# Graph attention layer: the pieces of a step stand in another order on TensorE, ScalarE and VectorE

## The chip, the cores and the metric

One NeuronCore of a Trainium2 chip runs the whole kernel. The metric is the device time of one execution in microseconds (us).

## The reference

Four graph layers run one after the other on 50,000 nodes of 128 features and 25,000 edges, sorted by their target. After each layer the result is added to the input and normalised. The change lies in the third layer, graph attention with four heads. For every edge, and for a self loop at every node:

```
x_l, x_r = x @ W_l + b_l, x @ W_r + b_r
m = leaky_relu(x_l[src] + x_r[tgt] + edge_weight @ W_e, 0.2)
logits = einsum('ehc,hc->eh', m, att)
ex = exp(logits - segment_max(logits, tgt)[tgt])
alpha = ex / (segment_sum(ex, tgt)[tgt] + 1e-16)
out = gelu(segment_sum(alpha * x_l[src], tgt) + bias)
h = out + x;  out = (h - mean) * rsqrt(var + eps) * ln_w + ln_b
x = layernorm(x + out)
```

## The kernel before

Each layer is a function with a program of its own for each engine; all engines meet at its end. `layer2` is the attention layer. It works on 49 tiles (`STEPS`) of 512 edges and, beside them, 49 tiles of 1024 nodes (two blocks of 512). Its loop counts steps `c` from 0 to 62 on each engine. In step `c` the engines handle edge and node tile `c` freshly gathered, node tile `g1 = c-1` and `g2 = c-2` in the later parts of the normalisation, and, 11 steps behind (`lag`), edge tiles `e0 = c-11`, `e1 = c-12`, `e2 = c-13`, whose attention weights are known by then. So there are three regimes: steps 0 to 11 without the edge tail (the ramp), steps 13 to 48 with everything, and steps 49 to 62 with the edge tail alone (the drain). Every seven tiles form a run, whose softmax is done in two steps: `s1` in steps 8, 15, 22, ..., 50 (`running_maximum`, `maximum_between_chunks`, `exponents`) and `s2` one step later (`running_sum`, `sum_between_chunks`, `weights`).

Every engine executes its program strictly in the order in which it is written, and waits on semaphores for the others. The order inside a step is written out by hand. In this document the pieces have these names; the line is that of the profile.

TensorE (PE): V, the value products of both edge ends (L1394, L1395, into psZ); A, the logits (L1405, L1406, into psA); TN, turning the node tile (L1361 from xn, into psT); EN and EE, centring of the gelu results of nodes and edges (L1366 into psP and psU); T1N and T1E, turning the normalised rows of nodes and edges (L1361 from n, into psT and psU); ZR and ZS, the products for the logits (L1444, L1446, into psZ); FN and FE, the second centring (L1366 into psP and psU); TE, turning the edge rows of the next tile (L1361 from xd_xs, into psT); Y, the node product (L1475, into psP). The run steps add small products into psA: m_rows, m_cols (s1), d_rows, d_cols (s2).

ScalarE (ACT): G and GE, gelu of nodes and edges (L1496, L1501, with a table load ahead); nodeT (L1505), values (L1509), alike (L1514), a table load back (L1516), affn and affe (L1520, L1525), sq (L1534), low (L1538), Exp (L1543, run steps), edgeT (L1486), lnv (L1549), rstd (L1553).

VectorE (DVE): N1, the scaling (L1567); W, S and AGG, weighting, adding and scanning of values (L1680, L1682, L1685); P1N and P1E, the residual additions that read EN and EE (L1694, L1699); ZW (L1711); VAR, the row sums (L1571); P2N and P2E, the additions that read FN and FE (L1728, L1746); Z, ZSL, ZL, the inputs of the logits (L1734, L1738, L1741).

The order of a step before:

```
PE   V A TN EN EE [m_rows d_rows] T1N T1E ZR ZS [m_cols d_cols] FN FE TE Y
ACT  G GE nodeT values alike table affn affe sq low [Exp] edgeT lnv rstd
DVE  N1 [max sum] W S AGG P1N P1E [between chunks] ZW VAR [exponents weights] P2N Z ZSL ZL P2E
```

The DMA queue of SyncE loads the edge weights, xn, share (each head's attention weights, spread over 32 partitions) and x2e, and stores logits, pre2 and shares. It is in order too: xn of tile c+1 waits for P2N of step c-1, share for AGG, the logits for alike. GpSimd gathers xd_xs, two tiles ahead of TE. `wait(eng, sem, n)` is a semaphore wait that is left out while n is not positive.

Of the kernel before, what the change touches and what calls it, by code (L numbers as in the profile page):

```python
# [20 lines left out]
P = 128  # L21
NODES, EDGES = 50000, 25000
TILE = 512
# [1187 lines left out]
def layer2(nc, io, h):  # L1211
# [4 lines left out]
    with ExitStack() as ctx:  # L1216
# [5 lines left out]
        lag, ring, runs = 11, 12, 7  # L1222
# [51 lines left out]
        def blocks_of(g):  # L1274
            return 0 if is_tile(g) else 2, 3 if is_tile(g - lag) else 2

        def is_group(g):
            return 0 <= g < STEPS + lag

        def run_at(c, behind):  # L1280
            s, k = divmod(c - behind, runs)
            return s if k == 0 and 0 <= s < runs else None
# [17 lines left out]
        def _(sp):  # L1300
# [15 lines left out]
            for c in range(ends):  # L1316
                if is_tile(c + 1):
                    load_weights(c + 1)
                    load_nodes(c + 1)
# [24 lines left out]
                g3, e3 = c - 3, c - 3 - lag  # L1344
# [13 lines left out]
        def _(pe):  # L1358
# [28 lines left out]
            for c in range(ends):  # L1387
                now, last = is_tile(c), is_tile(c - 1)
                g1, g2, e1, e2 = c - 1, c - 2, c - 1 - lag, c - 2 - lag
# [7 lines left out]
                if last:  # L1397
                    pe.wait_ge(zl_ready, c)
                    pe.wait_ge(zsl_ready, c)
                    wait(pe, a_kept, c - 1)  # L1400
                    done = (c - 1 - runs - 1) // runs + 1
                    wait(pe, m_cols, done)
                    done = (c - 1 - runs - 2) // runs + 1
                    wait(pe, d_cols, done)
                    nc.tensor.matmul(psA[0:36, 0, :], att_a[:, :], zl[:, :], start=True, stop=False)  # L1405
                    nc.tensor.matmul(psA[0:36, 0, :], att_s[:, :], zsl[:, :], start=False, stop=True).then_inc(a_ready, 1)  # L1406
                if now:
                    pe.wait_ge(node_landed[c % 4], 16 * (c // 4 + 1))
                    for k in range(2):
                        ins = turned_rows(psT[:, k, :], xn[:, c % 4, k, :])  # L1410
                    ins.then_inc(n_turned, 1)
# [9 lines left out]
                s = run_at(c, runs + 1)  # L1421
                if s is not None:
                    pe.wait_ge(top_done, s + 1)
                    pe.wait_ge(a_kept, min(c, STEPS))
                    rows_of(psA[:, 0, :], [m_here[:, chunk - 1:chunk]]).then_inc(m_rows, 1)
                s = run_at(c, runs + 2)
                if s is not None:
                    pe.wait_ge(sums_done, s + 1)
                    pe.wait_ge(a_kept, min(c, STEPS))
                    rows_of(psA[:, 0, :], [c_here[:, chunk - 1:chunk], d_here[:, chunk - 1:chunk]]).then_inc(d_rows, 1)  # L1430
                if is_group(g2):
                    pe.wait_ge(n1_ready, g2 + 1)
                if is_tile(g2):
                    pe.wait_ge(n_kept, min(c + 1, STEPS))
                    wait(pe, affn_ready, g2)
                    for k in range(2):
                        ins = turned_rows(psT[:, k, :], n1[:, k, :])
                    ins.then_inc(n1n_turned, 1)
                if is_tile(e2):
                    pe.wait_ge(pre1e_ready, min(e1 + 1, STEPS))  # L1440
                    turned_rows(psU[:, 0, :], n1[:, 2, :]).then_inc(n1e_turned, 1)
                if now:
# [3 lines left out]
                    nc.tensor.matmul(psZ[:, 1, :], h.w_lr[:, :], edgeT[:, c % 2, 0, :],  # L1446
                                     start=True, stop=True).then_inc(zs_ready, 1)
                s = run_at(c, runs + 1)
                if s is not None:
                    pe.wait_ge(m_lined, s + 1)  # L1450
                    nc.tensor.matmul(psA[:, 0, P:P + 1], m_line[:, :], ones[:, :], start=True, stop=True).then_inc(m_cols, 1)
                s = run_at(c, runs + 2)
                if s is not None:
                    pe.wait_ge(d_lined, s + 1)
                    nc.tensor.matmul(psA[:, 0, 2 * P:2 * P + 1], d_line[:, :], ones[:, :],
                                     start=True, stop=True).then_inc(d_cols, 1)
# [6 lines left out]
                if is_tile(e2):  # L1463
                    pe.wait_ge(affe_ready, e2 + 1)
                    centred(psU[:, 0, :], affT[:, 2, :]).then_inc(fe_ready, 1)
                if is_tile(c + 1):
                    pe.wait_ge(n_kept, c + 1)
                    wait(pe, affn_ready, g2 + 1)
                    turn_edges(c + 1)
                if now:  # L1470
                    pe.wait_ge(n_kept, c + 1)
                    wait(pe, pre1n_ready, g1 + 1)
                    wait(pe, pre2n_ready, g2 + 1)
                    for k in range(2):
                        ins = nc.tensor.matmul(psP[:, k, :], h.w["w_l"][:, :], nodeT[:, c % 2, k, :],  # L1475
                                               start=True, stop=True)
                    ins.then_inc(y_ready, 1)

        @block.scalar
        def _(act):  # L1480
# [9 lines left out]
            for c in range(ends):  # L1490
                now, last = is_tile(c), is_tile(c - 1)
                g1, g2, e1, e2 = c - 1, c - 2, c - 1 - lag, c - 2 - lag
# [9 lines left out]
                if now:  # L1502
                    act.wait_ge(n_turned, c + 1)
                    wait(act, y_ready, c - 1)
                    nc.scalar.activation(nodeT[:, c % 2, :, :], psT[:, :, :], ACT.Copy).then_inc(n_kept, 1)  # L1505
# [5 lines left out]
                if last:  # L1511
                    act.wait_ge(a_ready, c)
                    wait(act, alike_stored[(c - 1) % 2], 32 * ((c - 1) // 2))
                    nc.scalar.activation(alike[:, (c - 1) % 2, :], psA[0:36, 0, :], ACT.Copy).then_inc(a_kept, 1)  # L1514
# [7 lines left out]
                if is_tile(e2):  # L1522
                    act.wait_ge(n1e_turned, e2 + 1)
                    wait(act, ee_ready, min(e1 + 1, STEPS))
                    nc.scalar.activation(affT[:, 2, :], psU[:, 0, :], ACT.Identity, bias=h.col("ln_b"),  # L1525
                                         scale=h.col("ln_w")).then_inc(affe_ready, 1)
                if is_group(g1):
                    a, b = blocks_of(g1)
# [5 lines left out]
                    nc.scalar.activation(sq1[:, a:b, :], pre1[:, a:b, :], ACT.Square).then_inc(sq1_ready, 1)  # L1534
                if now:
# [4 lines left out]
                s = run_at(c, runs + 1)  # L1540
                if s is not None:
                    act.wait_ge(args_ready, s + 1)
                    nc.scalar.activation(expo[:, :, :], expo[:, :, :], ACT.Exp).then_inc(exps_ready, 1)  # L1543
                if is_tile(c + 1):
                    keep_edges(c + 1)
                if is_group(g1):
# [3 lines left out]
                                         scale=1.0 / P).then_inc(lnv1_ready, 1)  # L1550
                    act.wait_ge(lnv1_ready, g1 + 1)
                    wait(act, n1_ready, g1)
                    nc.scalar.activation(rstd1[:, 4 * a:4 * b], lnv1[:, 4 * a:4 * b], ACT.Exp,  # L1553
                                         scale=-0.5).then_inc(rstd1_ready, 1)

        @block.vector
        def _(dve):
# [104 lines left out]
            for c in range(ends):  # L1662
                now = is_tile(c)
                g1, g2, e0, e1, e2 = c - 1, c - 2, c - lag, c - 1 - lag, c - 2 - lag
                if is_group(g2):
                    a, b = blocks_of(g2)
# [3 lines left out]
                    scaled(n1[:, a:b, :], pre1[:, a:b, :], rstd1[:, 4 * a:4 * b], b - a, n1_ready)  # L1670
                s = run_at(c, runs + 1)
                if s is not None:
                    running_maximum(s)
                s = run_at(c, runs + 2)
                if s is not None:
                    running_sum(s)
                if is_tile(e0):
# [3 lines left out]
                    dve.wait_ge(weighed, e0 + 1)  # L1681
                    nc.vector.tensor_tensor(v[:, 0, :], v[:, 0, :], v[:, 1, :], ALU.add).then_inc(summed, 1)  # L1682
                    dve.wait_ge(summed, e0 + 1)
                    wait(dve, ge_ready, e0 - 1)
                    nc.vector.tensor_tensor_scan(agg[:, e0 % 2, :], share[:, e0 % 2, 0, :], v[:, 0, :],  # L1685
                                                 0.0 if e0 == 0 else agg[:, 1 - e0 % 2, TILE - 1:TILE],
                                                 ALU.mult, ALU.add).then_inc(agg_ready, 1)
                if is_group(g1):
                    wait(dve, n1_ready, g1)
                    wait(dve, sq1_ready, g1)  # L1690
                if is_tile(g1):
# [4 lines left out]
                if is_tile(e1):  # L1696
                    dve.wait_ge(ee_ready, e1 + 1)
                    dve.wait_ge(x2e_landed[e1 % 4], 16 * (e1 // 4 + 1))
                    nc.vector.tensor_tensor(pre1[:, 2, :], psU[:, 0, :], x2e[:, e1 % 4, :],  # L1699
                                            ALU.add).then_inc(pre1e_ready, 1)  # L1700
                s = run_at(c, runs + 1)
                if s is not None:
                    maximum_between_chunks(s)
# [381 lines left out]
```

## Time and profile before

| | |
|---|---|
| median of 3 runs | 3335.7 us (3334.68 to 3337.22) |
| the profiled execution | 3335.34 us, span 3333.5 us |
| attention layer | about 1797 to 2775 us of the span |
| mean granted TensorE clock | 0.903 |

Times in the rows are microseconds from the start of the span. A row of the timeline gives start, duration, engine, line, what is written from what, the number of instructions merged, and in brackets the idle time before it with what ended it. The duration of a group of matmuls includes the end of the last one; from the start of one group to the start of the next is what the engine needs for it. PEclk is the share of full speed (2.4 GHz) that the throttle granted.

### The profile page before, as it was taken

How to read it: one execution, taken by the hardware profiler on the slowest of the kernel's cores; microseconds unless marked ns; L12 is line 12 of the kernel's file. 1: busy time of each engine (PE TensorE's matmuls, PEld its weight loads, DVE VectorE, ACT ScalarE, POOL GpSimd, SP SyncE). 2: the span in 40 equal slices, each digit the busy share in tenths (PEclk: the TensorE clock that was granted, in tenths of full speed). 3: DMA queues.
4: the chain of work that ended last, by engine and by line, in shares of the span. 5: the costliest groups of instructions: out<-in, count | busy, mean ns of one | idle time of the engine just before them, and what ended most of it. 6: DMA issues, size and time to landing. Idle time of an engine off the chain costs nothing. (4 is left out here: it accounts for less than half of the span.)

```text
span 3333.5 us, 45939 instructions
## 1 busy us (share of the span) xinstructions
PE 2612.3 (78%) x14227; PEld 1767.1 (53%) x14227; DVE 2674.7 (80%) x3290; ACT 2007.4 (60%) x3334; POOL 1912.3 (57%) x1771
## 2 busy tenths in 40 slices
PE   7899999869999968888886989999999853435510
PEld 3466666646666646656654556666666642224300
DVE  6599999969999969999995467788778765999910
ACT  0177777646556649899895666666766653545500
POOL 4477777433333337777773555555555105777776
PEclk9999999989999989999997999999999955566855
DMA  7467667556666647777774456776776656985211
GB/s 209 111 191 221 221 220 222 190 179 199 201 197 198 198 152 230 229 235 231 230 237 122 121 147 172 191 181 178 193 183 178 161 130 194 280 275 172 84 39 40
DMA packets 495084, 611.76 MB, mean 184 GB/s; under 512 B 66866, under 2 KB 284652, under 8 KB 494717
## 3 DMA queue, kind: packets, MB, share of 16 engines
q1 hardware_dynamic: 433030, 495.63, 49.1%
q0 software_dynamic: 56480, 111.88, 12.7%
q8 instruction: 118, 1.93, 0.2%
q10 hardware_dynamic: 5334, 1.32, 0.2%
q14 instruction: 122, 0.99, 0.1%
HBM read 391.94 MB, written 220.55 MB: 184 GB/s over the span
## 5 line engine op out<-in xcount | busy, mean ns | idle before, releaser
L1294 POOL DMA_INDIRECT g_xd_xs<-table_x,dst_row x196 | 227.8, 1162 | 338.8 <-PE g_psT L1361 245.7
L1801 POOL DMA_INDIRECT f_rows<-table_x,src_row x196 | 229.2, 1169 | 231.9 <-POOLq L1216 172.5
L775 POOL DMA_INDIRECT c_xs<-table_x,src_row x196 | 185.4, 946 | 303.4 <-PE c_psT L916 250.2
L765 POOL DMA_INDIRECT c_xs<-table_h,src_row x196 | 220.5, 1125 | 120.5 <-issue 78.4
L497 POOL DMA_INDIRECT xs<-in_x,src_i x196 | 227.1, 1159 | 86.5 <-issue 55.5
L482 POOL DMA_INDIRECT xd<-in_x,dst_i x196 | 216.6, 1105 | 94.8 <-issue 47.9
L1294 POOL DMA_INDIRECT g_xd_xs<-table_x,src_row x196 | 221.0, 1128 | 59.8 <-issue 59.8
L1808 POOL DMA_INDIRECT out<-f_rows,end_i x196 | 197.4, 1007 | 62.5 <-issue 62.5
L1853 PE MATMUL f_psT<-w_ident,f_rows 128*128 128x128 f32 x196 | 48.7, 395 | 220.3 <-DVE f_rows L1946 220.3
L765 POOL DMA_INDIRECT c_xd<-table_h,dst_row x196 | 185.8, 948 | 59.8 <-issue 59.8
L1366 PEld LDWEIGHTS g_psP<-w_center,g_turns 128*128 128x128 f32 x1568 | 185.5, 192 | 26.6 <-ACT g_turns L1520 13.1
L1571 DVE TENSOR_REDUCE g_var<-g_sq 128x12 f32<-128x1536 f32 (+2 forms) x60 | 87.6, 1460 | 139.1 <-ACT g_sq L1534 136.4
L1366 PE MATMUL g_psP<-w_center,g_turns 128*128 128x128 f32 x1568 | 194.2, 277 | 5.8 <-ACT g_turns L1520 5.8
L1023 ACT ACTIVATE c_xo<-c_pre,c_rstd 128x128 f32<-128x128 f32 x588 | 181.9, 388 | 1.6
L1853 PEld LDWEIGHTS f_psT<-w_ident,f_rows 128*128 128x128 f32 x196 | 31.0, 195 | 233.1 <-DVE f_rows L1946 233.1
L1366 PE MATMUL g_psU<-w_center,g_turns 128*128 128x128 f32 x784 | 125.2, 311 | 34.7 <-ACT g_turns L1501 23.3
L1694 DVE TENSOR_TENSOR g_pre<-g_psP,g_xn 128x1024 f32<-128x1024 f32 x49 | 60.0, 1224 | 107.4 <-PE g_psP L1366 107.4
L1070 ACT ACTIVATE c_xnT<-c_psT 128x512 f32<-128x512 f32 x196 | 111.5, 599 | 40.6 <-PE c_psT L916 40.2
L1505 ACT ACTIVATE g_nodeT<-g_psT 128x1024 f32<-128x1024 f32 x49 | 50.2, 1024 | 141.6 <-PE g_psT L1361 141.6
L1366 PEld LDWEIGHTS g_psU<-w_center,g_turns 128*128 128x128 f32 x784 | 112.5, 221 | 41.9 <-ACT g_turns L1501 28.8
L946 PE MATMUL c_psV<-c_xsT,w_v 128*128 128x512 f32 x196 | 105.8, 622 | 35.6 <-DVE c_pv L1162 35.6
L1877 ACT ACTIVATE f_sqe<-f_rows 128x512 f32<-128x512 f32 x49 | 30.8, 629 | 166.9 <-DVE f_vare L1923 146.5
(333 smaller groups left out, 8643.8 us busy)
## 6 DMA issues: line engine op xcount, KB each, us to landing
g_share<-shares SPq DMA_DIRECT2D x196, 192.0 KB
xn<-in_x SPq DMA_DIRECT2D x49, 512.0 KB
table_x<-xo SPq DMA_DIRECT2D x49, 512.0 KB
table_x1b<-xb SPq DMA_DIRECT2D x49, 512.0 KB, 4.9
c_xn<-table_x SPq DMA_DIRECT2D x49, 512.0 KB
table_h<-c_xo SPq DMA_DIRECT2D x49, 512.0 KB
c_xn<-table_h SPq DMA_DIRECT2D x49, 512.0 KB
c_x1r<-table_x1b SPq DMA_DIRECT2D x49, 512.0 KB
```

Source lines behind the costliest of these rows:

```text
L482: pool.indirect_dma_start(out=quarters(h.xd0[:, s, :])[j], out_offset=None, in_=io["x0"], in_offset=edge_index(h.dst_i, n, j)).then_inc(h. ...
L497: pool.indirect_dma_start(out=quarters(h.xs0[:, s, :])[j], out_offset=None, in_=io["x0"], in_offset=edge_index(h.src_i, n, j)).then_inc(h. ...
L765: pool.indirect_dma_start(out=quarters(rows[:, s, :])[j], out_offset=None, in_=table, in_offset=edge_index(columns, now.n, j)).then_inc(la ...
L775: pool.indirect_dma_start(out=quarters(xs[:, s, :])[j], out_offset=None, in_=table, in_offset=edge_index(h.src_row, now.n, j)).then_inc(sr ...
L946: nc.tensor.matmul(psV[:, :], w_v[:, :], xsT[:, now.slot, :], start=True, stop=True).then_inc(v_ready, 1)
L1023: ins = nc.scalar.activation(quarters(xo[:, g.slot, j // 4, :])[j % 4], quarters(pre[:, g.slot, j // 4, :])[j % 4], ACT.Copy, scale=rstd[: ...
L1070: nc.scalar.activation(xnT[:, s, k, :], psT[0 if spread else k][:, :], ACT.Copy).then_inc(turned_sb, 1)
L1294: pool.indirect_dma_start(out=quarters(xd_xs[:, s, k, :])[j], out_offset=None, in_=table, in_offset=edge_index(columns, now.n, j)).then_in ...
L1366: ins = nc.tensor.matmul(o, x, h.w["center"][:, :], start=True, stop=True)
L1571: nc.vector.tensor_reduce(var, by_row(sq.rearrange("p b n -> p (b n)")), AX_X, ALU.add).then_inc(ready, 1)
L1801: pool.indirect_dma_start(out=quarters(rows[:, n, :])[j], out_offset=None, in_=table, in_offset=edge_index(h.src_row, n, j)).then_inc(src_ ...
L1808: pool.indirect_dma_start(out=io["out"], out_offset=edge_index(h.end_i, n, j), in_=quarters(rows[:, n, :])[j], in_offset=None, bounds_chec ...
```

## The change

The same instructions are issued in another order. `behind` is 0, so `d` is `c`, `lead` is `lag`, and which tile is handled in which step stays.

```
PE   V TN EN EE T1N ZR A FN T1E ZS [m_rows d_rows] TE FE [m_cols] Y [d_cols]
ACT  G GE nodeT values table affn sq alike affe low lnv edgeT rstd [Exp]
DVE  N1 W [max sum] P1N ZW P1E Z S ZL VAR P2N [between chunks] ZSL [exponents] AGG P2E [weights]
```

Waits that were implied by the old order are written out: TN waits for edgeT and affn (readers of psT), T1E for N1, TE for affn; A waits for `args_ready` and `shares_ready` (VectorE has read psA) where it waited for `m_cols` and `d_cols` (TensorE has written it); ZL waits for A of its own step. The core of the diff:

```diff
-        lag, ring, runs = 11, 12, 7
+        lag, ring, runs, behind = 11, 12, 7, 0
+        lead = lag - behind
...
@@ sync @@
                 if is_tile(c + 1):
                     load_weights(c + 1)
-                    load_nodes(c + 1)
+                if is_tile(c + 1 - behind) and c + 1 > behind:
+                    load_nodes(c + 1 - behind)
...
@@ tensor @@
-                if last:
-                    pe.wait_ge(zl_ready, c)
-                    pe.wait_ge(zsl_ready, c)
-                    wait(pe, a_kept, c - 1)
...
-                    wait(pe, m_cols, done)
...
-                    wait(pe, d_cols, done)
-                    nc.tensor.matmul(psA[0:36, 0, :], att_a[:, :], zl[:, :], start=True, stop=False)
-                    nc.tensor.matmul(psA[0:36, 0, :], att_s[:, :], zsl[:, :], start=False, stop=True).then_inc(a_ready, 1)
-                if now:
-                    pe.wait_ge(node_landed[c % 4], 16 * (c // 4 + 1))
+                if is_tile(d):
+                    pe.wait_ge(node_landed[d % 4], 16 * (d // 4 + 1))
+                    pe.wait_ge(e_kept, min(c + 1, STEPS))
+                    wait(pe, affn_ready, min(g2, STEPS))
...
-                if is_tile(e2):
-                    pe.wait_ge(pre1e_ready, min(e1 + 1, STEPS))
-                    turned_rows(psU[:, 0, :], n1[:, 2, :]).then_inc(n1e_turned, 1)
                 if now:
                     pe.wait_ge(v_kept, c + 1)
                     nc.tensor.matmul(psZ[:, 0, :], h.w["w_r"][:, :], edgeT[:, c % 2, 0, :],
                                      start=True, stop=True).then_inc(z_ready, 1)
...
+                if last:
+                    pe.wait_ge(zl_ready, c)
+                    pe.wait_ge(zsl_ready, c)
+                    wait(pe, a_kept, c - 1)
...
+                    wait(pe, args_ready, done)
...
+                    wait(pe, shares_ready, done)
+                    nc.tensor.matmul(psA[0:36, 0, :], att_a[:, :], zl[:, :], start=True, stop=False)
+                    nc.tensor.matmul(psA[0:36, 0, :], att_s[:, :], zsl[:, :], start=False, stop=True).then_inc(a_ready, 1)
...
                 if is_tile(e2):
+                    pe.wait_ge(n1_ready, g2 + 1)
+                    pe.wait_ge(pre1e_ready, min(e1 + 1, STEPS))
+                    turned_rows(psU[:, 0, :], n1[:, 2, :]).then_inc(n1e_turned, 1)
+                if now:
+                    pe.wait_ge(v_kept, c + 1)
+                    nc.tensor.matmul(psZ[:, 1, :], h.w_lr[:, :], edgeT[:, c % 2, 0, :],
+                                     start=True, stop=True).then_inc(zs_ready, 1)
...
+                if is_tile(c + 1):
+                    wait(pe, n_kept, min(d + 1, STEPS))
+                    wait(pe, affn_ready, min(g2 + 1, STEPS))
+                    turn_edges(c + 1)
+                if is_tile(e2):
                     pe.wait_ge(affe_ready, e2 + 1)
                     centred(psU[:, 0, :], affT[:, 2, :]).then_inc(fe_ready, 1)
...
@@ vector @@
+                if now:
+                    dve.wait_ge(z_added, c + 1)
+                    wait(dve, a_ready, c)
+                    nc.vector.scalar_tensor_tensor(out=zl[:, :], in0=z[:, :], scalar=0.2, in1=z[:, :],
+                                                   op0=ALU.mult, op1=ALU.max).then_inc(zl_ready, 1)
                 if is_group(g1):
...
                     sums(var1[:, 4 * a:4 * b], sq1[:, a:b, :], var1_ready)
...
+                if is_tile(e0):
+                    v = values[:, e0 % ring, :, :]
+                    dve.wait_ge(summed, e0 + 1)
+                    wait(dve, ge_ready, e0 - 1)
+                    nc.vector.tensor_tensor_scan(agg[:, e0 % 2, :], share[:, e0 % 2, 0, :], v[:, 0, :],
```

The rest of the diff moves the other pieces to the places shown in the order above, with their waits.

## Rows read from the trace of the kernel before

**Rows 1.** Windows: stretch, length, busy PE, PEld, DVE, ACT, POOL, PEclk, DMA share, GB/s.
```profile
2010.00:2620.00 610.00, 571.74 (x3236) 381.70 (x3237) 477.99 (x583) 419.55 (x492) 327.67 (x272) 1.00 0.72 182
2660.00:2772.00 112.00, 64.11 (x258) 51.96 (x258) 67.61 (x99) 55.00 (x77) 0.00 (x0) 0.53 0.43 113
```

**Rows 2.** Timeline of TensorE, two neighbouring plain steps, from T1E to T1N.
```profile
2217.21 0.66 PE L1361 MATMUL g_psU<-w_ident,g_n 128*128 128x128 f32 x4 [0.32 <-DVE g_pre L1699]
2217.70 1.02 PE L1444 MATMUL g_psZ<-g_edgeT,w_w_r 128*128 128x512 f32 x2
...
2219.42 1.95 PE L1366 MATMUL g_psP<-w_center,g_turns 128*128 128x128 f32 x16
...
2222.10 1.04 PE L1361 MATMUL g_psT<-w_ident,g_xd_xs 128*128 128x128 f32 x8
...
2223.49 1.96 PE L1475 MATMUL g_psP<-g_nodeT,w_w_l 128*128 128x512 f32 x4 [0.36 <-DVE g_pre L1728]
...
2225.36 1.10 PE L1394 MATMUL g_psZ<-g_edgeT,w_w_l 128*128 128x512 f32 x2
...
2227.25 1.05 PE L1405 MATMUL g_psA<-g_zl,g_att_a 128*36 128x512 f32 x2
...
2229.09 1.09 PE L1361 MATMUL g_psT<-w_ident,g_xn 128*128 128x128 f32 x8
...
2230.01 1.95 PE L1366 MATMUL g_psP<-w_center,g_turns 128*128 128x128 f32 x16
...
2231.80 1.06 PE L1366 MATMUL g_psU<-w_center,g_turns 128*128 128x128 f32 x8
...
2232.70 1.04 PE L1361 MATMUL g_psT<-w_ident,g_n 128*128 128x128 f32 x8
```

**Rows 3.** Timeline of ScalarE and VectorE in the same two steps.
```profile
2217.19 1.21 ACT L1520 ACTIVATE g_turns<-g_psT,cols 128x1024 f32<-128x1024 f32 x1
...
2218.95 1.48 ACT L1534 ACTIVATE g_sq<-g_pre 128x1536 f32<-128x1536 f32 x1
...
2220.46 1.75 DVE L1571 TENSOR_REDUCE g_var<-g_sq 128x12 f32<-128x1536 f32 x1 [2.65 <-ACT g_sq L1534]
...
2224.58 0.68 DVE L1741 SCALAR_TENSOR_TENSOR g_zl<-g_z 128x512 f32<-128x512 f32 x1
```

**Rows 4.** Waits from 2005 to 2625 us: total, times, longest.
```profile
DVE g_var L1571 <- ACT g_sq L1534: 86.4, 36, 2.7
...
PE g_psP L1475 <- DVE g_pre L1728: 31.4, 35, 2.6
```

**Rows 5.** Timeline: V of steps 2, 8, 22 and 24.
```profile
1838.51 1.10 PE L1394 MATMUL g_psZ<-g_edgeT,w_w_l 128*128 128x512 f32 x2 [1.49 <-DVE g_zl L1741]
...
1930.29 1.10 PE L1394 MATMUL g_psZ<-g_edgeT,w_w_l 128*128 128x512 f32 x2
...
2170.06 1.10 PE L1394 MATMUL g_psZ<-g_edgeT,w_w_l 128*128 128x512 f32 x2
...
2208.52 1.10 PE L1394 MATMUL g_psZ<-g_edgeT,w_w_l 128*128 128x512 f32 x2
```

**Rows 6.** Timeline: V of step 10, and Y of step 16.
```profile
1965.51 1.10 PE L1394 MATMUL g_psZ<-g_edgeT,w_w_l 128*128 128x512 f32 x2
...
2082.57 3.52 PE L1475 MATMUL g_psP<-g_nodeT,w_w_l 128*128 128x512 f32 x4 [2.43 <-DVE g_pre L1728]
```

**Rows 7.** Timeline of one plain drain step: GE, AGG and the next GE.
```profile
2729.37 0.72 ACT L1501 ACTIVATE g_turns<-g_agg,cols 128x512 f32<-128x512 f32 x1
...
2731.29 1.28 DVE L1685 TENSOR_TENSOR_SCAN g_agg<-g_share,g_agg,g_values 128x512 f32<-128x512 f32 x1
...
2738.70 0.72 ACT L1501 ACTIVATE g_turns<-g_agg,cols 128x512 f32<-128x512 f32 x1
```

**Rows 8.** Windows of two earlier layers, same columns as Rows 1.
```profile
320.00:360.00 40.00, 40.00 (x214) 27.23 (x213) 39.40 (x36) 27.64 (x36) 31.77 (x28) 1.00 0.69 217
1480.00:1520.00 40.00, 34.52 (x203) 24.46 (x203) 38.44 (x52) 35.57 (x84) 28.69 (x28) 1.00 0.71 223
```

More of the change, by code:

```diff
@@ L1445, in _ @@
                                      start=True, stop=True).then_inc(z_ready, 1)
[L1446 to L1456, printed above, removed]
+                if last:
+                    pe.wait_ge(zl_ready, c)
+                    pe.wait_ge(zsl_ready, c)
+                    wait(pe, a_kept, c - 1)
+                    done = (c - 1 - runs - 1) // runs + 1
+                    wait(pe, args_ready, done)
+                    done = (c - 1 - runs - 2) // runs + 1
+                    wait(pe, shares_ready, done)
+                    nc.tensor.matmul(psA[0:36, 0, :], att_a[:, :], zl[:, :], start=True, stop=False)
+                    nc.tensor.matmul(psA[0:36, 0, :], att_s[:, :], zsl[:, :], start=False, stop=True).then_inc(a_ready, 1)
                 if is_tile(g2):
@@ L1501, in _ @@
                     nc.scalar.activation(ge[:, :], agg[:, e1 % 2, :], ACT.Gelu, bias=h.col("g_bias")).then_inc(ge_ready, 1)
[L1502 to L1505, printed above, removed]
+                if is_tile(d):
+                    act.wait_ge(n_turned, d + 1)
+                    wait(act, y_ready, d - 1)
+                    nc.scalar.activation(nodeT[:, d % 2, :, :], psT[:, :, :], ACT.Copy).then_inc(n_kept, 1)
                 if now:
@@ L1539, in _ @@
                                          scale=0.2).then_inc(low_ready, 1)
[L1540 to L1545, printed above, removed]
                 if is_group(g1):
@@ L1554, in _ @@
                                          scale=-0.5).then_inc(rstd1_ready, 1)
+                if s1 is not None:
+                    act.wait_ge(args_ready, s1 + 1)
+                    nc.scalar.activation(expo[:, :, :], expo[:, :, :], ACT.Exp).then_inc(exps_ready, 1)
         @block.vector
@@ L1669, in _ @@
                     wait(dve, n1e_turned, e2)
[L1670 to L1676, printed above, removed]
+                    scaled(n1[:, a2:b2, :], pre1[:, a2:b2, :], rstd1[:, 4 * a2:4 * b2], b2 - a2, n1_ready)
                 if is_tile(e0):
@@ L1680, in _ @@
                     nc.vector.tensor_tensor(v, v, share[:, e0 % 2, 1:3, :], ALU.mult).then_inc(weighed, 1)
[L1681 to L1688, printed above, removed]
+                if s1 is not None:
+                    running_maximum(s1)
+                if s2 is not None:
+                    running_sum(s2)
+                if is_tile(g1):
                     wait(dve, n1_ready, g1)
                     wait(dve, sq1_ready, g1)
-                if is_tile(g1):
                     dve.wait_ge(en_ready, g1 + 1)
@@ L1695, in _ @@
                                             ALU.add).then_inc(pre1n_ready, 1)
[L1696 to L1703, printed above, removed]
-                s = run_at(c, runs + 2)
-                if s is not None:
-                    sum_between_chunks(s)
                 if now:
@@ L1747, in _ @@
                                             ALU.add).then_inc(pre2e_ready, 1)
+                if s2 is not None:
+                    weights(s2)
 def layer3(nc, io, h):
```

138 lines of the change are left out of this document (77 added, 61 removed).

## The prediction

> **What bounds the kernel now.** I read the windows first, to see which engine is full in the attention layer while all its parts run: TensorE is busy 94% of the stretch from 2010 to 2610 us, VectorE 78%, ScalarE 69%, GpSimd 54%, the DMA engines 72% [rows 1]. Then the timeline of two plain steps, to see whether TensorE is the bound or only nearly. A step lasts from V at 2208.52 to V at 2225.36, 16.84 us [rows 2, 5]. The starts give what each piece needs: T1E 0.49, ZR and ZS 1.72, FN and FE 2.68, Y 1.87, V 1.89, A 1.84, TN 0.92, EN 1.79, EE 0.90 [rows 2]. TE and T1N are eight turnings like TN, so 0.90 each. The sum is 15.90, and 0.94 is left: from TE to Y pass 1.39 instead of 0.90, and the rest lies ahead of T1E, whose row has idle time behind P1E [rows 2]. Last the waits: Y stands for P2N (31.4 us in 35 steps, 0.9 each on average), and VAR stands 2.4 us in each step for sq [rows 4]. So the step is a loop through all three engines: EN, P1N, P1E, T1E, affe, sq, VAR, P2N, Z, ZSL, ZL, and V of the next step, which starts 0.10 us after ZL has ended at 2225.26 [rows 2, 3]. TensorE is almost, not quite, the bound. In the steps with a softmax run the loop is longer, because the extra VectorE work stands inside it: steps 22 and 23 together take 2208.52 - 2170.06 = 38.46, not 33.68 [rows 5]. In the drain TensorE is busy 57% and its granted clock is 0.53 of full, which is the lower level (1.2 GHz) nearly throughout [rows 1]; the loop there is GE, EE, P1E, T1E, affe, FE, a table load, GE: 9.33 us [rows 7].
>
> **The change, worked out.** No instruction is added or removed, so what can change is the waiting alone. I walk a plain step in the new order, with time 0 at V and the durations of the rows.
>
> TensorE, if it never waits: V 0, TN 1.9, EN 2.8, EE 4.6, T1N 5.5, ZR 6.4, A 7.3, FN 9.1, T1E 10.9, ZS 11.4, TE 12.2, FE 13.1, Y 14.0, next V 15.9 (ZR and ZS are 0.86 each, FN 1.79 like EN, FE 0.90 like EE [rows 2]). Now whether each input is there.
>
> ScalarE: TN has ended at 3.0, nodeT runs to 4.0 and values to 5.1 (ZR wants it at 6.4, T1N wants nodeT at 5.5). The table load runs to 6.3, T1N ends at 6.5, affn takes 1.21 [rows 3] and ends at 7.8 (FN at 9.1). sq takes 1.48 [rows 3] and ends at 9.2. alike follows A to 9.8. affe follows T1E (11.5) to 12.3 (FE at 13.1). low follows ZS (12.4) to 13.1, then lnv, edgeT to 14.4 (V at 15.9), rstd, table load to 15.9; G follows Y (16.0) to 17.2, which is 1.3 of the next step (EN at 2.8).
>
> VectorE: P1N after EN, 4.8 to 6.0; ZW to 6.7, P1E to 7.3, Z, S to 8.8; ZL waits 0.4 for A and ends at 9.9; VAR takes 1.75 [rows 3] to 11.5 and has sq ready before it, where it stood 2.4 us; P2N to 12.7 (Y at 14.0); ZSL follows low to 13.9, AGG to 15.1, P2E to 15.7, N1 to 17.4, which is 1.5 of the next step (T1N at 5.5).
>
> Each input is early, the tightest by 0.8 us (affe for FE). So the step becomes TensorE's own 15.90, and the gain is 0.94. The loop is cut where it mattered: VAR no longer stands behind affe, ZL no longer behind P2N, and V finds ZL and ZSL two microseconds old. The durations without a row of their own are 0.7 for a 512-column operation and 1.2 for a 1024-column one, as ZL and affn [rows 3]; VectorE and ScalarE have room in total, since 78% and 69% of 16.84 to 17.5 us are 13.7 and 12.0 [rows 1].
>
> What moves later, with its cover: alike by 2.4 us and with it the logits' store and, once a run, the load of packed; the DMA queue then stands for alike while xn, share and x2e of the step have been issued. AGG moves from early in the step to its end, 15.1, so share is asked for at about the place where P2N lets the queue through now; W wants it more than a step later. weights moves behind P2E, so the shares' store and everything queued behind it (edge weights, xn, share, x2e) start some 3 us later once a run, against 15 us until TN wants xn. GpSimd waits for TE, which comes earlier, and has 46% of the time free [rows 1]. If one of these covers were gone, a transfer late by t would cost t in that step alone.
>
> Written-out waits: TN's for edgeT and affn, T1E's for N1 and A's for exponents and weights name work that ended microseconds before, by the walk. Their bounds are nothing and the 0.10 us between ZL's end and V [rows 2, 3], at which a wait that is just met passes. I take 0.1 us a step, 5 us in all, since pieces also get new neighbours.
>
> The sum:
> - Plain full steps: 49 to 12 leaves steps 13 to 48, 36, of which 10 hold runs. 26 times 0.94 is 24.4.
> - Five pairs of run steps. TensorE's extra products are single ones of one tile; by T1E's 0.49 for four turnings I put them at 1.4 a pair, and 0.3 for a stall of m_cols behind `maximum_between_chunks`. New 31.8 + 1.7 = 33.5, old 38.46 [rows 5]: 5.0 each, 24.8. In the s1 step args_ready comes at 16.3, Exp and the table load push G to 19.2, 2.7 of the next step: just ahead of EN at 2.8. weights push N1 to 4.2 of the step after s2 (T1N at 5.5). Bounds of a pair: 3.5 (both just miss) and 5.3.
> - The gap of 2.43 us ahead of Y in step 16 let the clock fall, and Y took 3.52 instead of 1.96 [rows 2, 6]. Without it: 1.5.
> - Ramp: no EE, T1E and FE, so 15.90 - 2.3 = 13.6, against (1930.29 - 1838.51) / 6 = 15.30 [rows 5]. The walk holds there too; T1N comes at 4.6 with nodeT at 4.0, V at 13.6 with edgeT at 13.1. 1.7 for each of steps 2 to 7, 10, 11 and, by estimate, 12 and 1: 17.0, less 0.7 for the unsure last two: 16.3.
> - Steps 8 and 9: 1965.51 - 1930.29 = 35.2 [rows 5, 6] against 27.2 + 1.7: 6.3.
> - Drain: EE lasts 2.1 at the low clock, so P1E could start some 2.9 after GE, but waits for AGG, which ends at 2732.57, 3.2 after GE [rows 7]. With P1E ahead of AGG a step saves 0.25: 1.8 for steps 53 to 59. Steps 49 to 52 mix both regimes: estimated 4, bounds 0 and 6.
>
> Together 24.4 + 24.8 + 1.5 + 16.3 + 6.3 + 5.8 = 79.1, less 5 for the waits: 74. The profiled execution took 3335.34, 0.4 below the median of 3335.7, so I predict 3335.7 - 74 = 3262 us.
>
> **The clock.** A fully packed TensorE keeps its full clock in this trace: in the first layer it is busy 40.00 of 40 us at 1.00 [rows 8]. In sentences that the rest can do without: the Trainium skill (TensorE: Matmul & The Clock Gate, section A second HAM failure mode: psum-queue depth-cycling) tells of a kernel whose small idle times between groups that cycle through the banks kept the clock oscillating. By that rule this layer would swing between the levels; the trace disagrees so far, with 1.00 over 610 us of exactly such groups [rows 1].
>
> **The rivals.**
> - Half a gain (0.16): one input I hold early is late by about 0.5 us a step (affe for FE, or G behind Exp), for 49 steps and 10 more in run steps: 74 - 34 = 40, so 3296. For it: the margins of 0.8 and 0.1. Against it: the durations repeat to a hundredth from step to step.
> - The loop only changes its members and stays at 16.84: 3335, no change (0.04). For it: three engines in order are coupled as before. Against it: by the walk V would have to wait, and its inputs are there 1.5 us early.
> - Slower: AGG, P2E and N1 now stand behind ZSL, which stands for low and ZS, the tenth piece. If that tail ends more than 4 us late, T1N stands. Only run steps add such lateness (exponents 1.6, weights 2.5); to eat the gain each of the 14 would have to lose 5.3 us, and at 6.5 the time is 3352 (0.04). Against it: both are not in one step.
> - The clock swings (0.03): the packed stretch of some 750 us is at TensorE's pace; with a tenth of it at the lower level it grows by 75 and the time is 3337. This is what the page's rule of above would do here.
> - DMA as the bound is no rival of weight: the step at 15.9 asks for 0.72 x 16.84 / 15.9 = 0.76 and 193 GB/s, and a layer before runs at 223 GB/s [rows 8].
>
> **How the numbers follow.** The forecast has 0.73: its own range is 74 + 14 and 74 - 22 (0.15 us a step either way, the bounds of pairs and drain): 3248 to 3284. The range for 8 in 10 reaches a little up to the first rival: 3245 to 3290. Only a difference over 0.2% (7 us) can be told from no change. Faster 0.90, within 0.2% 0.04, slower 0.06 (the third rival, and half of the clock's).
>
> **What would show it.** V to V 15.9 to 16.0 in plain steps and 13.6 in the ramp; TensorE over 99% busy with PEclk 1.00 from 1990 to 2580; Y's wait for P2N and VAR's for sq gone, ZSL waiting for low and ZL for A instead; a pair of run steps at 33.5; drain steps at 9.1. Wrong would be: a new wait of TensorE at FE, EN or T1N in each step, a lower PEclk, or a step ruled by another chain.

## The result, and the profile after

The changed kernel takes 3251.84 us in the median (3250.13 to 3254.27, 4 runs) against 3336.11 us (3334.68 to 3337.22, 4 runs): a ratio of 0.9748, 95% interval 0.9731 to 0.9765. The forecast was 3262 with 3245 to 3290, so the case that was held likeliest came, 10 us better than its number. The profiled execution took 3252.72 us (span 3250.9), 82.6 us less than that of before; the accounts below are made between these two.

The windows of the attention layer after, columns as in [rows 1]: the full stretch, and the drain.

```profile
1990.00:2540.00 550.00, 549.13 (x3224) 379.24 (x3223) 471.09 (x578) 425.02 (x487) 317.59 (x271) 1.00 0.82 202
```
```profile
2600.00:2690.00 90.00, 49.42 (x192) 40.20 (x192) 51.13 (x69) 45.58 (x64) 0.00 (x0) 0.51 0.47 113
```

TensorE has 549.13 of 550 us full and keeps the clock at 1.00; before it was 571.74 of 610 [rows 1]. So the change turned a loop through three engines into a step of TensorE alone. The DMA share is 0.82 (predicted 0.76), and no row of TensorE in this stretch stands for a transfer. Now one plain step on TensorE, from V to V:

```profile
2197.08 1.02 PE L1398 MATMUL g_psZ<-g_edgeT,w_w_l 128*128 128x512 f32 x2
...
2198.80 1.04 PE L1363 MATMUL g_psT<-w_ident,g_xn 128*128 128x128 f32 x8
2199.67 1.95 PE L1368 MATMUL g_psP<-w_center,g_turns 128*128 128x128 f32 x16
...
2203.22 1.02 PE L1426 MATMUL g_psZ<-g_edgeT,w_w_r 128*128 128x512 f32 x2
2204.18 1.05 PE L1436 MATMUL g_psA<-g_zl,g_att_a 128*36 128x512 f32 x2
2205.07 1.02 PE L1437 MATMUL g_psA<-g_zsl,g_att_s 128*36 128x512 f32 x2
2206.02 2.05 PE L1368 MATMUL g_psP<-w_center,g_turns 128*128 128x128 f32 x16
2207.91 0.60 PE L1363 MATMUL g_psU<-w_ident,g_n 128*128 128x128 f32 x4
...
2210.97 1.88 PE L1475 MATMUL g_psP<-g_nodeT,w_w_l 128*128 128x512 f32 x4
```

The next V starts at 2212.69, so the step is 15.61 us where 15.90 was predicted, and no row has a bracket: TensorE never waits in it. What waits instead, from the view of waits, 2005 to 2500 us (total, times, longest):

```profile
ACT g_turns L1538 <- PE g_psU L1363: 56.1, 31, 1.8
DVE g_pre L1691 <- PE g_psP L1368: 39.0, 22, 2.0
...
PEld g_psA L1436 <- issue: 23.5, 31, 0.8
...
DVE g_zl L1720 <- PE g_psA L1437: 14.3, 27, 0.6
DVE g_zsl L1738 <- ACT g_low L1543: 9.1, 21, 0.4
...
PE g_psP L1368 <- ACT g_turns L1502: 0.9, 5, 0.2
```

Y's wait for P2N and VAR's for sq [rows 4] are gone; TensorE's own waits (the last line) are 0.9 us in 495. In a plain step ScalarE stands 1.8 us for TensorE ahead of affe, and VectorE 2.0 ahead of P1N and 0.56 ahead of ZL; ZSL stands 0.43 for low, which ScalarE makes of TensorE's ZS. That is what engines that are not the bound look like.

**Where the 82.6 us came from**, by the starts of V in both traces (V of step 0 at 1813.06 and 1813.37, of step 48 at 2627.07 and 2548.19):

| part | predicted | measured |
|---|---|---|
| 25 plain steps among 13 to 47 | 23.5 (0.94 each) | 30.3 (16.84 - 15.61 = 1.23 each, less 0.10 in the step behind each of five pairs) |
| five run pairs | 24.8 | 23.8 (38.46 - 33.69 = 4.77 each) |
| low clock of step 16 | 1.5 | 1.5 (that pair 39.92, the other four 38.46) |
| ramp without steps 8, 9 | 16.3 | 18.1 (13.38 a step, predicted 13.6) |
| steps 8 and 9 | 6.3 | 5.5 |
| step 48 and the drain | 6.7 | 3.7 |
| waits, start of step 0 | -5 | -0.3 |
| sum | 74.1 | 82.6 |

### The profile page after: what moved, and what is told of

Read it like the earlier page. It is cut to its first block and busy times, and to the rows that moved or that the text cites. A ratio compares the mean times of both kernels' runs of the same rounds, so it can differ in the third digit from the quotient of the medians.

```text
span 3250.9 us, 46100 instructions
## 1 busy us (share of the span) xinstructions
PE 2585.9 (80%) x14227; PEld 1765.5 (54%) x14227; DVE 2676.2 (82%) x3290; ACT 2016.0 (62%) x3334; POOL 1900.7 (58%) x1771
## 5 line engine op out<-in xcount | busy, mean ns | idle before, releaser
L1295 POOL DMA_INDIRECT g_xd_xs<-table_x,dst_row x196 | 243.4, 1242 | 271.6 <-PE g_psT L1363 179.8
L1295 POOL DMA_INDIRECT g_xd_xs<-table_x,src_row x196 | 195.2, 996 | 59.7 <-issue 59.7
L1136 DVE TENSOR_TENSOR_SCAN c_m<-far,c_m,c_psA 128x512 f32<-128x512 bf16 x98 | 124.8, 1273 | 0.5 <-PE c_psA L951 0.5
L1089 ACT ACTIVATE c_xo<-c_pre 128x1024 f32<-128x1024 f32 x49 | 51.8, 1057 | 115.0 <-DVE c_pre L1193 115.0
```

Of the source, the lines that this page charges most:

```text
L1136: nc.vector.tensor_tensor_scan(m[:, s, 1:TILE + 1], h.far[:, here], psA[:, :], m[:, s, 0:1], ALU.add, ALU.max).then_inc(m_ready, 1)
L1295: pool.indirect_dma_start(out=quarters(xd_xs[:, s, k, :])[j], out_offset=None, in_=table, in_offset=edge_index(columns, now.n, j)).then_in ...
```

## Experiments

The runs were made in three sessions, each with the kernel before beside them. In two of them that kernel takes 3335 to 3336 us. In the third, on another chip, it takes 3548 us, and TensorE stands at times that the others don't show; below this is "the slow chip". Times are compared within a session, by ratio.

**What is left at TensorE: the narrow weights of A.** In the step above ZR takes 0.96 from start to start where ZS takes 0.86, A 1.84 and FN 1.89 where EN takes 1.79. Ahead of A and ahead of FN TensorE loses 0.10. A is the only piece of a plain step whose weights (the operand that is loaded into the array ahead of the product) have 36 columns and not 128.

```diff
-        att_a, att_s = sb("att_a", [P, 36]), sb("att_s", [P, 36])
+        att_a, att_s = sb("att_a", [P, P]), sb("att_s", [P, P])
...
-                    nc.tensor.matmul(psA[0:36, 0, :], att_a[:, :], zl[:, :], start=True, stop=False)
+                    nc.tensor.matmul(psA[:, 0, :], att_a[:, :], zl[:, :], start=True, stop=False)
```

(and the same for `att_s`; the new columns are zero.) First on the slow chip:

> The changed kernel with the weights of A widened from 36 to 128 columns (92 of them zero), everything else the same. In every step of both kernels 0.10 us are lost ahead of A and 0.11 behind it, and no weights are loaded ahead there. Theory X (this comes of the 36 column weights): both vanish, 0.2 us a step, 49 steps: about 3242. Theory Y (it comes of the waits ahead of A and of the piece behind it): 3252. Theory Z (wider weights cost their loading): 3254 to 3260.

Measured: 3468.18 us, ratio 0.9764 (0.973 to 0.9797). Its undisturbed steps take 15.29 to 15.39, but every other one some 16.8, so the total can't decide. On a usual chip, beside the changed kernel as a control:

> The changed kernel as it is, on the chip of the next three: a ratio to the kernel before of 0.975, a plain step of 15.61 us. It tells what the chip does to the others of this call.

> The weights of A widened to 128 columns, again, beside the changed kernel on the same chip. If the 0.1 us ahead of A and behind it come of the 36 column weights: plain step 15.39, some 10 us under the changed kernel, if no other stall takes it back. If steps of 16.8 us alternate with 15.39 here too, the wide form causes them, and the time is that of the changed kernel or above it.

Measured: control 3251.03 us, ratio 0.9749 (0.9736 to 0.9763); wide A 3235.4 us, ratio 0.9704 (0.9691 to 0.9717), 15.6 us under the control and more than expected. The weight loads (PEld) and matmuls around A, wide:

```profile
2195.05 0.19 PEld L1436 LDWEIGHTS g_psA<-g_zl,g_att_a 128*128 128x128 f32 x1 [0.24 <-issue]
...
2196.76 0.19 PEld L1368 LDWEIGHTS g_psP<-w_center,g_turns 128*128 128x128 f32 x1 [0.24 <-issue]
```
```profile
2194.61 1.02 PE L1426 MATMUL g_psZ<-g_edgeT,w_w_r 128*128 128x512 f32 x2
2195.48 1.02 PE L1436 MATMUL g_psA<-g_zl,g_att_a 128*128 128x512 f32 x2
2196.33 1.02 PE L1437 MATMUL g_psA<-g_zsl,g_att_s 128*128 128x512 f32 x2
2197.19 1.95 PE L1368 MATMUL g_psP<-w_center,g_turns 128*128 128x128 f32 x16
2198.98 0.60 PE L1363 MATMUL g_psU<-w_ident,g_n 128*128 128x128 f32 x4
```

And the loads of the changed kernel:

```profile
2204.18 0.14 PEld L1436 LDWEIGHTS g_psA<-g_zl,g_att_a 128*36 128x36 f32 x2 [0.76 <-issue]
2204.64 0.11 PEld L1437 LDWEIGHTS g_psA<-g_zsl,g_att_s 128*36 128x36 f32 x1 [0.32 <-issue]
...
2206.01 1.08 PEld L1368 LDWEIGHTS g_psP<-w_center,g_turns 128*128 128x128 f32 x9 [0.83 <-issue]
```

Wide, A's weights are loaded at 2195.05, 0.43 ahead of the matmul that uses them, under the matmul of ZR; narrow, the load and the matmul both stand at 2204.18. FN's load too comes 0.43 early behind a wide A and not at all early behind a narrow one. Between the two narrow products it does come early: the load of `att_s` starts at 2204.64, its matmul at 2205.07. The step goes from 15.61 to 15.29: 0.09 at ZR, 0.13 in A, 0.10 at FN. The Trainium skill (TensorE: Matmul & The Clock Gate, section Architectural detail: the array is 16× 32×32, not 1× 128×128) says that TensorE's queue can pull weight loads ahead of matmuls in flight. By these rows that holds between weights of one width, and not where 128 columns change to 36 or 36 to 128. The edit also makes the result of A 128 rows high instead of 36, and the two were not changed apart; that it is the weights is read from the starts of the loads. This version is faster than both kernels of the case.

Is TensorE's slack in the kernel before real? The same edit there:

> The kernel before with A's weights widened from 36 to 128 columns (zeros in the new ones; the same logits come out). In the changed kernel that gave 0.32 us a step. Theory (before, the step is a loop through three engines and TensorE has slack): the step stays near 16.84, and only what of A lies in the loop counts, since V's inputs come from ZL, which waits for P2N and not for A: 0 to 4 us of gain, 3331 to 3336. Rival (TensorE was the bound before as well, and its small idle times are part of it): the same 0.32 in each of 49 steps, 15 us, 3320.

Measured: 3325.63 us against 3335.86, ratio 0.9971 (0.9961 to 0.9981), 10.2 us less; the plain step went from 16.84 to 16.57 and the ramp step from 15.32 to 15.05. Both expectations miss. The loop of before is V, A, TN, EN, P1N, P1E, T1E, affe, sq, VAR, P2N, Z, ZSL, ZL, V: my walk began it at EN, but V, A and TN stand between V's inputs and EN on TensorE, so A is in the loop though TensorE waits elsewhere. The 0.27 is 0.10 in V, 0.12 in A and 0.05 in TN, all ahead of EN. A microsecond of an engine with slack still counts where the engine's order puts it into the loop. The gain of the kernel is smaller than 0.27 in every step, because in three of the four run pairs from step 22 on Y now runs at the low clock behind the same 2.60 us of standing as before, which costs 1.5 us each time:

```profile
2320.03 3.65 PE L1475 MATMUL g_psP<-g_nodeT,w_w_l 128*128 128x512 f32 x4 [2.60 <-DVE g_pre L1728]
```

In the kernel before the four Ys in these places took 1.95 or 1.96.

**Which engine's order carries the gain.** Each kernel here is the changed one with one engine's plain pieces in the order of before. ScalarE:

```diff
+                if last:
+                    act.wait_ge(a_ready, c)
...
+                if is_tile(e2):
+                    act.wait_ge(n1e_turned, e2 + 1)
```

(alike goes ahead of the table load and affn, affe ahead of sq, edgeT and Exp ahead of lnv.)

> The changed kernel with ScalarE's step alone in the order of before (alike ahead of the table load and affn, affe ahead of sq). Theory (the new orders hold each other up: TensorE's new order is packed only because alike no longer stands ahead of affn): alike waits for A, which now ends at about 8.8 of the step, so affn ends at 11.9 instead of 7.5, FN starts there, T1E at 13.7, sq ends at 16.5, VAR at 18.2, P2N at 19.4, Y starts at 19.5: a plain step of about 21.2 us, a ramp step of 16.0, in all about 3480 us, slower than the kernel before. Rival (TensorE's order alone carries the gain): 3252 to 3270.

Measured on the slow chip: 3818.63 us, ratio 1.0744 (1.0697 to 1.0791), a plain step of 23.88. The direction holds and the size is larger: ScalarE stands for A, with affn behind it, and TensorE for affn. First ScalarE, then TensorE, then the window behind:

```profile
2378.06 0.59 ACT L1520 ACTIVATE g_alike<-g_psA 36x512 f32<-36x512 f32 x1 [4.22 <-PE g_psA L1437]
```
```profile
2381.22 3.78 PE L1368 MATMUL g_psP<-w_center,g_turns 128*128 128x128 f32 x16 [3.20 <-ACT g_turns L1526]
2384.80 1.06 PE L1363 MATMUL g_psU<-w_ident,g_n 128*128 128x128 f32 x4
2385.65 1.74 PE L1450 MATMUL g_psZ<-g_edgeT,w_lr 128*128 128x512 f32 x2
```
```profile
2381.00:2387.00 6.00, 5.78 (x22) 5.00 (x23) 0.00 (x0) 1.27 (x3) 0.00 (x0) 0.50 0.48 129
```

What the walk of 21.2 us left out is the clock. During the stand of 3.20 us the granted clock falls to 0.50, and FN takes 3.58 and T1E 0.85 from start to start where they take 1.89 and 0.43 in the changed kernel. Both stand ahead of affe, sq, VAR and P2N, and Y waits for P2N, so this is 2.1 of the 2.7 us over the walk. Whether the slow chip added the rest was not told apart. VectorE (S and AGG back behind W, ZW behind P1E, Z and ZL behind P2N):

> The changed kernel with VectorE's plain pieces in the order of before (S and AGG behind W, P1E ahead of ZW, VAR and P2N ahead of Z, ZSL, ZL); the run pieces keep their new places. Theory (TensorE alone is the bound now and VectorE has two microseconds to spare): by the walk VAR ends at 10.9, P2N at 12.3, ZL at 14.5, N1 at 1.2 of the next step, so the plain step stays 15.6 us, run steps within 0.3, the drain loses the 0.25 a step again: 3250 to 3258. Rival (each engine's order carries a share of the gain, VectorE's the largest since ZL and VAR ended the loop of before): a plain step of 16.2 or more and over 3275.

Measured there: 3466.38 us, ratio 0.9781 (0.9748 to 0.9813). The plain steps are 15.61, as expected: VectorE's order is not needed in them. Its run pairs take 36.6 us where the wide-A kernel has 33.4 on the same chip (V at 2554.27 and 2587.63) and the changed kernel 33.69 on the others, with TensorE standing for G ahead of EN in each:

```profile
2319.93 2.05 PE L1368 MATMUL g_psP<-w_center,g_turns 128*128 128x128 f32 x16 [1.42 <-ACT g_turns L1502]
```

So the new order of VectorE does seem to earn some 3 us a pair, in the run steps alone. That part was not expected, and since the changed kernel itself was not run on that chip, it is not shown beyond doubt. TensorE, on the slow chip and again on a usual one:

```diff
+                if last:
+                    pe.wait_ge(zl_ready, c)
...
+                    nc.tensor.matmul(psA[0:36, 0, :], att_a[:, :], zl[:, :], start=True, stop=False)
...
+                if is_tile(g2):
+                    pe.wait_ge(affn_ready, g2 + 1)
```

(V A TN EN EE T1N T1E ZR ZS FN FE TE Y.)

> The changed kernel with TensorE's plain pieces in the order of before (A behind V, T1E ahead of ZR, FE ahead of TE); the run products keep their new places and waits. Theory (the loop is cut on TensorE): T1E waits for P1E until 9.0, VAR ends at 14.3 because Z, S, ZL stand ahead of it, P2N at 15.5, Y starts at 15.6, a plain step of about 17.3; ramp step 14.3; in all 3330 to 3350, no gain over the kernel before. Rival (the orders of ScalarE and VectorE carry the gain): under 3290.

> The changed kernel with TensorE's plain pieces in the order of before, on a chip where TensorE does not stall. On the other chip the plain step was 18.33 us and the ratio 1.0115. Theory (the two elementwise engines' new orders need TensorE's new order: each serves the other; the stalls of that chip added nothing to a loop that is not TensorE's): the ratio is again 1.00 to 1.02, 3340 to 3400, with a plain step of 17.9 to 18.4. Rival (the step of 18.33 was that chip's stalls, and the walked value of 17.3 holds): 3320 to 3340, a plain step of 17.2 to 17.5.

Measured: 3589.87 us and 1.0115 (1.0087 to 1.0143) on the slow chip, with a step of 18.33; 3348.09 us and 1.0039 (1.0023 to 1.0054) on the usual one, with 17.57. So the first expectation (3330 to 3350, 17.3) was right on an undisturbed chip, 0.76 us a step was added on that chip. Of the second expectation the time range holds, but its step of 17.9 to 18.4, and with it the claim that the chip added nothing, is wrong; its rival's 17.2 to 17.5 is close. Two waits that the new order has not are back in each step, by the timeline on the usual chip:

```profile
2252.25 0.63 PE L1363 MATMUL g_psU<-w_ident,g_n 128*128 128x128 f32 x4 [1.07 <-DVE g_pre L1705]
...
2258.67 1.95 PE L1475 MATMUL g_psP<-g_nodeT,w_w_l 128*128 128x512 f32 x4 [0.52 <-DVE g_pre L1729]
```

T1E stands straight behind T1N and waits for P1E, as in [rows 2]; Y waits for P2N. Without TensorE's new order the other two orders lose all the gain and 12 us. So the new orders of TensorE and of ScalarE are both needed; what either brings with the other two engines in the old order was not run.

**Why a pair of run steps cost 38.46.** The prediction put the extra VectorE work inside the loop. So more of it was added, in the kernel before and in the changed one:

```diff
                 link(nc.vector.tensor_scalar(den[:, :], den[:, :], DEN_EPS, None, ALU.add))
+                link(nc.vector.tensor_scalar(den[:, :], den[:, :], DEN_EPS, None, ALU.add))
...
```

> The kernel before, with the link in weights that adds DEN_EPS repeated five times more (about 0.26 us each with its link, 1.3 us in all, once a run, in the s2 step). It asks why a pair of run steps cost 38.46 us before. Theory (the extra VectorE work of a run stands inside the loop through the three engines): each of the seven runs gets 1.3 us longer, less what lies in the drain, so about 7 to 9 us over the kernel before: 3343 to 3345 on a chip where that takes 3335.5, and a pair in the middle of the layer goes from 38.46 to about 39.8. Rival (the run steps were long for TensorE's extra products and the extra transfers): nothing, 3335 to 3337.

> The same five links in the changed kernel. Theory (weights now stands behind P2E, and what it pushes, N1 and P1N of the next step, has over a microsecond to spare): 0 to 2 us over the changed kernel, 3251 to 3253, with a pair of run steps at 33.7. Rival (weights is still in the path of the step, with VectorE as the second bound): 7 to 9 us, 3258 to 3260, and a pair at 35.0.

Measured: 3354.18 us against 3335.86, ratio 1.0059 (1.0046 to 1.0073), 18.3 us more; and 3256.12 us, ratio 0.9761 (0.9748 to 0.9775), 4.3 to 5.1 us above the changed kernel's medians in two other sessions. The work is in the loop before and mostly out of it after, but both sizes were underrated. Before, the s2 step went from 19.79 to 22.72 and the next from 16.84 to 17.50. Y of the lengthened s2 step of before, then the windows around it:

```profile
2210.20 3.75 PE L1475 MATMUL g_psP<-g_nodeT,w_w_l 128*128 128x512 f32 x4 [3.84 <-DVE g_pre L1733]
2213.75 1.76 PE L1394 MATMUL g_psZ<-g_edgeT,w_w_l 128*128 128x512 f32 x2
```
```profile
2207.00:2208.00 1.00, 0.00 (x0) 0.00 (x0) 0.97 (x2) 0.95 (x4) 0.86 (x1) 1.00 0.00 0
2208.00:2209.00 1.00, 0.00 (x0) 0.00 (x0) 0.93 (x4) 1.00 (x1) 0.69 (x2) 0.70 0.24 66
2209.00:2210.00 1.00, 0.00 (x0) 0.00 (x0) 1.00 (x2) 0.16 (x1) 0.70 (x2) 0.50 0.13 37
...
2214.00:2215.00 1.00, 1.00 (x2) 0.42 (x2) 1.00 (x2) 1.00 (x1) 1.00 (x1) 0.50 1.08 275
2215.00:2216.00 1.00, 1.00 (x3) 0.19 (x1) 0.96 (x2) 0.72 (x2) 0.69 (x2) 0.89 1.13 174
```

The wait grew by the added 1.24 us (3.84 for 2.60), but while TensorE stood, the granted clock fell to 0.50 (1.2 GHz), and came back at 2215. Y then took 3.55 to V instead of 1.87 and V 1.59 to its second product instead of 0.94: 1.68 and 0.65 on top. It is the same thing as in step 16 of before [rows 6], now in each of the four later run pairs as well. So of the 3.6 us that such a pair grew by, 1.24 are the added work and 2.3 the clock. In the changed kernel weights pushes N1, and T1N, which had 1.1 us to spare behind it, misses it by a little:

```profile
2172.47 1.09 PE L1363 MATMUL g_psT<-w_ident,g_n 128*128 128x128 f32 x8 [0.19 <-DVE g_n L1572]
```

The step behind a pair takes 16.12 for 15.71 then: 0.4 of the 1.3 us comes through, and 1.1 in step 10, where the ramp is.

**The ramp.** `behind` delays the node pieces by so many steps, so that the first steps hold edge pieces alone and the drain gets the nodes (`behind = 4`, then `behind = 11`, one line).

> The changed kernel with behind = 4: the node tiles run four steps later, so four ramp steps hold edges alone and four drain steps hold nodes too. Theory (TensorE is the bound in the ramp, waits are in the drain, so work moved from the one to the other is hidden): ramp steps of 10.6 instead of 13.4, since GpSimd needs 10.3 for a tile, drain steps with nodes of 11.5 instead of 9.2 at the full clock: 3250 plus or minus 5. Rival (the node work fills idle time of the drain for nothing): 3240.

> The same with behind = 11, all ramp steps without nodes. By the first theory 11 times 2.8 less in the ramp, 11 times 2.3 more in the drain: 3246 plus or minus 12. By the rival 3222.

Measured: 3253.72 us, ratio 0.9754 (0.974 to 0.9769), and 3260.85, ratio 0.9778 (0.9763 to 0.9793): the first the same as the control within the intervals, as the theory had it; the second slower by 9.8 us, above what either side expected. With 4, V of step 48 comes 13.8 us sooner and the rest takes 14.2 longer; with 11 it is 32.8 sooner and 43.2 longer. In the changed kernel TensorE is full in the ramp:

```profile
1841.00:1900.00 59.00, 59.00 (x320) 37.92 (x319) 34.03 (x36) 46.63 (x54) 37.95 (x39) 1.00 0.44 126
```

With 11 the ramp steps shrink from 13.38 only to 9.9 to 10.5 us. TensorE then waits for ScalarE's edgeT, which follows TE, and TE waits for the gathered rows:

```profile
1829.67 1.12 PE L1398 MATMUL g_psZ<-g_edgeT,w_w_l 128*128 128x512 f32 x2 [1.11 <-ACT g_edgeT L1490]
...
1837.91 1.06 PE L1363 MATMUL g_psT<-w_ident,g_xd_xs 128*128 128x128 f32 x8 [1.03 <-DMA g_xd_xs<-table_x,src_row]
```
```profile
1836.52 0.94 POOL L1295 DMA_INDIRECT g_xd_xs<-table_x,dst_row  x1 [0.30 <-issue]
...
1846.51 1.35 POOL L1295 DMA_INDIRECT g_xd_xs<-table_x,dst_row  x1 [0.30 <-issue]
```

GpSimd issues eight gathers a tile, one every 1.25 us or a little more, without waiting for another engine for longer than the usual 0.30: 9.99 us between the two rows, which start neighbouring tiles. It is the bound there, as the expectation's 10.3 for a tile had it. Each drain step with nodes takes 12.66 (FN at 2641.81 and 2654.47) instead of 9.30, though TensorE's clock is 0.99 there:

```profile
2600.00:2690.00 90.00, 68.18 (x487) 56.74 (x486) 65.29 (x59) 59.31 (x67) 0.00 (x0) 0.99 0.52 148
```

So the nodes cost 3.4 us a step in the drain, where TensorE is busy 76% and no engine is full, and 3.2 in the ramp: moving them gains nothing. Why the whole drain of the second kernel costs 10 us more than its ramp saves was not followed further.

## Why the prediction was right

**The bound.** "TensorE is almost, not quite, the bound", and the loop as the cause of the 0.94 us a step: right. TensorE is full after, and with its own order undone the step is 17.57. The list of what is in the loop was short by V, A and TN, which changes no number of the prediction. (The stretch that it calls 2010 to 2610 is the 610 us from 2010 to 2620 [rows 1].)

**The step.** Walked: 15.90, and 0.1 for waits. Measured: 15.61. The terms that were mis-sized most are V and Y, taken as 1.89 and 1.87, while each is four products of 0.43, 1.72, in the step above. Y's 1.87 was read from its start to V's, and V stood for ZL there; and the first product behind a wait took 0.08 longer, in Y (1.96 where it lasts 1.88 now) and in V (its first half 1.10 [rows 2], now 1.02). The other 0.09 of V's 1.89 are the border to A's narrow weights: with a wide A the V of before takes 1.79. That border did not go away with the new order. It costs 0.10 at ZR (0.96) and 0.10 at FN (1.89) now, for which the walk had 0.86 and 1.79; small pieces make up the rest. A duration read behind a wait holds the cost of that wait's end, and one read up to the next piece's start holds that piece's wait. The 5 us for waits cost nothing that can be seen.

**The sum.** The 82.6 us are 8.5 more than the 74.1: 6.8 from plain steps, 1.8 from the ramp and 4.7 from the waits that didn't come, less 1.0 in run pairs, 0.8 in steps 8 and 9 and 3.0 in the drain. That the misses partly cancel is luck.

**The inputs.** Each was early, as walked, and ZL waits for A and ZSL for low, as predicted. The tightest, affe, ends 0.76 ahead of FE (2209.32 and 2210.08), where 0.8 was walked. The waits that were written out cost nothing that the rows show.

**Run steps.** 33.69 a pair against 33.5, which is closer than its terms: two plain steps are 31.2 and not 31.8, and what a run adds is 2.5 (0.96 in the s1 step, 1.52 in the s2 step) and not 1.7. The tight place was named: G behind Exp, "just ahead of EN". It misses by a little in the s2 step:

```profile
2151.57 2.05 PE L1368 MATMUL g_psP<-w_center,g_turns 128*128 128x128 f32 x16 [0.17 <-ACT g_turns L1502]
```

TN to EN is 1.21 there instead of 0.87. The single products cost d_rows 0.53 and d_cols 0.30, and the pieces next to them up to 0.1 each. The gap of step 16 and its clock are gone, as predicted.

**The ramp** followed the step: 13.38, which is 15.61 less EE, T1E and FE (0.89, 0.43, 0.89).

**The drain** was wrong. With P1E ahead of AGG a step was to save 0.25; it saves 0.03 (9.30 against 9.33 [rows 7]). GE and P1E, after:

```profile
2647.70 0.72 ACT L1507 ACTIVATE g_turns<-g_agg,cols 128x512 f32<-128x512 f32 x1
...
2650.76 0.69 DVE L1705 TENSOR_TENSOR g_pre<-g_psU,g_x2e 128x512 f32<-128x512 f32 x1 [1.90 <-PE g_psU L1368]
```

P1E starts 3.06 behind GE, before 3.12, and not at 2.9: EE ends 2.86 behind GE in both, and P1E starts 0.20 behind the end of EE, which the prediction left out. AGG had been in the way by 0.06 us. So the step of the prediction that failed here is the 0.25 a drain step. Steps 49 to 52 gave about 2.6 where 4 was estimated: EE of step 50 is 81.5 us earlier than before (2576.81 against 2658.33), and V of step 48 was 78.9 earlier. FN of step 50 then runs at the low clock, 3.78 us.

**The rivals.** None came. Against the clock's swinging stands the window above: 1.00 over 550 us of TensorE's groups with some 0.1 us lost between a few of them. The page named for that rival (the Trainium skill, TensorE: Matmul & The Clock Gate, section A second HAM failure mode: psum-queue depth-cycling) tells of a kernel whose clock oscillated through small idle times between groups of matmuls; by that rule the time would have been about 3337, and the trace disagrees. DMA stayed out at a share of 0.82. On the slow chip TensorE did stand, and there the ratio of the wide-A kernel is 0.9764 against 0.9704.

## What to carry to other kernels

When three ordered engines feed each other, walk one step with every input's time and look for pieces that stand straight behind their producer (T1E behind P1E, VAR behind sq): another piece of the same engine between them turns a wait into work, and the step falls to the fullest engine's own time. Take each duration from a place where neither the piece nor the one behind it waits, or the floor comes out too high. Once an engine is full, look at its own rows from start to start: here a 36-column weight among 128-column ones cost 0.32 us in each step, which widening it gave back.

## What the runs showed of the hardware

- Where the weights' width changes from 128 to 36 columns or back, the next load starts with its matmul and not 0.43 us ahead of it; within the pair of narrow products it starts ahead. This costs 0.32 us a step for one pair of narrow products, 15.6 us in the kernel.
- The length of TensorE's stand alone does not decide whether the granted clock falls to 0.50. Ahead of Y in the run steps, 2.60 us let it fall in none of four places in the kernel before, and in three of the same four in that kernel with a wide A; 2.43 us in step 16 did [rows 6], and 3.84 us did each time. With ScalarE in the old order 3.20 us did in the row at 2381.22 and in most steps around it, though not in all.
- The fall costs 1.5 us (step 16 of before) to 2.3 us (the lengthened s2 steps of before), there more than the added length of the stand, 1.24.
- In edge-only ramp steps GpSimd issues a gather every 1.25 us, eight a tile, and holds the step at 9.9 to 10.5 us.
- On one chip the kernel before ran in 3548 us, in the other sessions in 3335 to 3336, and TensorE stood there at times. What stands in the way there was not looked into.
